# Two mixture-of-experts layers of sixteen experts: from computing every expert to computing sorted 128-slot blocks

## The reference, cut to what matters

```
router_logits = x @ gate_w.T                      # 16 experts
topk_w, topk_idx = top_k(softmax(router_logits), 4)
combine = one_hot(topk_idx) * topk_w / sum(topk_w)
shared = (silu(x @ sg.T) * (x @ su.T)) @ shared_down.T * sigmoid(x @ shared_gate_vec.T)   # inner width 704
for e in range(16):                               # inner width 176 each
    h = silu(x @ g[e].T) * (x @ u[e].T)
    acc += (h @ d[e].T) * combine[:, e]
x = x + 0.5 * (shared + acc)
```

## Time and profile before

| | |
|---|---|
| three runs | 1092.65, 1092.97 and 1095.82 us, median 1092.97 |
| span of the profiled execution | 1092.5 us; the page gives no other time of that execution |
| busy | PE 1010.5, DVE 800.6, ACT 384.8, POOL 465.1 us |
| DMA | 27.38 MB, mean 25 GB/s |
| mean granted TensorE clock | 0.987 |

### The profile page before, as it was taken

How to read it: one execution, slowest core, us unless ns; L and a number is a source line. 1 busy time by engine, 2 the same in 40 slices (tenths; PEclk the granted TensorE clock), 3 DMA queues, 4 the chain that set the end, 5 groups by cost and what they waited for, 6 DMA issues and landing times.

```text
span 1092.5 us, 18432 instructions
## 1 busy us (share of the span) xinstructions
PE 1010.5 (92%) x6692; PEld 584.0 (53%) x6692; DVE 800.6 (73%) x1429; ACT 384.8 (35%) x615; POOL 465.1 (43%) x373
## 2 busy tenths in 40 slices
PE   3989999899899899899799999999999999999997
PEld 1546555455555455555356555554455544555554
DVE  6887776967876967878977786466888778885444
ACT  1223223366423356422232332324432344322332
POOL 3646743466523456525466622231342313422222
PEclk8989999999999999999999999999999999999999
DMA  5212310000000000001233100000000000000000
GB/s 172 87 59 88 101 59 1 1 1 1 1 1 1 1 1 2 1 1 53 64 108 102 44 1 1 0 1 1 1 1 1 1 1 1 1 1 20 1 0 19
DMA packets 11814, 27.38 MB, mean 25 GB/s; under 512 B 1720, under 2 KB 4024, under 8 KB 11744
## 3 DMA queue, kind: packets, MB, share of 16 engines
q1 hardware_dynamic: 11744, 26.44, 8.1%
HBM read 25.38 MB, written 1.05 MB: 24 GB/s over the span
## 4 chain that ended last, share of the span: by engine, by line
PE 51%; DVE 28%; issue 10%; POOL 7%; ACT 3%; DMA 1%; SPq 0%; DVEq 0%; POOLq 0%; ACTq 0%
PE ps L719 28%; PE ps L748 12%; DVE hid L935 4%; POOL hlo L515 3%; DVE hid L937 3%; DVE hid L931 3%; PE ps L730 3%; PE ps L861 2%; POOL scr L554 2%; DVE scr L1119 1%; PE ps L795 1%; PE ps L760 1%; DVE combine L1041 1%; DVE scr L1112 1%; DVE picked L1024 1%
## 5 line engine op out<-in xcount | busy, mean ns | idle before, releaser
L515 POOL TENSOR_TENSOR hlo<-hid,hhi 128x512 f16<-128x512 f32 x208 | 252.2, 1212 | 566.5 <-ACT hhi L592 566.5
L719 PE MATMUL ps<-xhi,whi 128*128 128x512 f16 x832 | 319.7, 384 | 26.1 <-DVE hid L931 25.6
L719 PE MATMUL ps<-xhi,wlo 128*128 128x512 f16 x832 | 319.2, 384 | 0.0
L719 PE MATMUL ps<-xlo,whi 128*128 128x512 f16 x832 | 319.1, 384 | 0.0
L592 ACT ACTIVATE hhi<-hid 128x512 f16<-128x512 f32 x208 | 130.9, 629 | 464.9 <-DVE hid L937 464.7
L931 DVE SCALAR_TENSOR_TENSOR hid<-gtanh,ps 128x512 f32<-128x512 f32 x208 | 142.2, 684 | 174.1 <-ACT gtanh L585 159.6
L748 PE MATMUL ps<-whi,hhi 128*128 128x256 f16 (+1 forms) x832 | 227.7, 274 | 0.8 <-POOL hlo L515 0.8
L748 PE MATMUL ps<-whi,hlo 128*128 128x256 f16 (+1 forms) x832 | 227.3, 273 | 0.0
L748 PE MATMUL ps<-wlo,hhi 128*128 128x256 f16 (+1 forms) x832 | 227.1, 273 | 0.0
L935 DVE TENSOR_TENSOR hid<-hid,ps 128x512 f32<-128x512 f32 x208 | 143.0, 687 | 61.0 <-PE ps L730 56.1
L585 ACT ACTIVATE gtanh<-ps 128x512 f32<-128x512 f32 x208 | 123.3, 593 | 104.7 <-PE ps L719 104.4
(11 more groups left out here) (164 smaller groups left out, 927.4 us busy)
## 6 DMA issues: line engine op xcount, KB each, us to landing
stage<-w_in SPq DMA_DIRECT2D x58, 384.0 KB, 3.1
out<-x SPq DMA_DIRECT2D x2, 512.0 KB, 3.1
sel<-sel_in SPq DMA_DIRECT2D x1, 672.0 KB, 7.7
sel<-sel_in SPq DMA_DIRECT2D x2, 288.0 KB, 3.6
x<-x_in SPq DMA_DIRECT2D x4, 128.0 KB, 2.6
x<-x_in SPq DMA_DIRECT2D x1, 512.0 KB, 8.4
const<-const_in SPq DMA_DIRECT2D x1, 128.0 KB, 2.4
rw<-rw_in SPq DMA_DIRECT2D x1, 64.0 KB, 2.2
```

The source lines that it names most:

```text
L515: pool.tensor_tensor(hlo[:, k, :], hid[:, k % 2, :], hhi[:, k, :], ALU.subtract).then_inc(lo_done, 1)
L719: mm = pe.matmul(ps[:, bank, :], w[:, ds(off, P)], a[:, kc, t0:t0 + HN], start=(n == 0), stop=(n == 3 * KC - 1))
```

## The change

The sixteen experts of L0 are no longer computed for all tokens. For each half (512 tokens, 4 experts each, 2048 pairs) the kernel sorts pairs by expert into slots: an expert gets as many blocks of 128 slots as it needs, and 31 blocks always hold them (`NBLK`). The eight dense passes become twelve: "shared" passes of 6 chunks (the shared expert alone, dense as before but without the selection product), "routed" passes of 31 blocks, and four dense L1 passes of 24 chunks as before. Their order is shared(L0, half 0), routed(0), routed(1), shared(1); then, for the second L0, shared(0), routed(0), shared(1), routed(1); then the four L1 passes. They are called S0, R0, R1, S1, S2, R2, S3, R3 and F0 to F3 below.

On the way, in order: POOL and ACT split the normed rows (`xr`); DVE finds the four chosen experts (`route_pick`); PE counts with a triangle of ones the place of each pair within its expert (`rank`); DVE turns that into a slot number (`place`), into each block's expert (`block_experts`) and into each pair's weight (`slot_weights`); 16 indirect DMAs from POOL (4 experts x 4 tiles of 128 tokens, `send`) write the rows into `xs_dram`, which was blanked at the start; SP reads each block back with a transposing DMA, six ahead; PE reads the block's expert from memory into a register and computes gate and up with the block's slots as the stationary side; after the block's hidden values, two PE transposes, a copy on ACT and a difference on DVE (`turn`); six down products; a copy on ACT and a store to `ys_dram` by SP. At last 16 indirect DMAs from POOL (`gather`) fetch the four rows of each token back, and DVE adds them with their weights (`combine`).

```diff
+NBLK = HN * K0 // P + E0 - 1
+XRING, YRING, GRING = 6, 3, 4
-FFN_STAGES = (0, 2, 3, 5)
+PASSES = [(SH, 0, 0), (RT, 0, 0), (RT, 0, 1), (SH, 0, 1), (SH, 2, 0), (RT, 2, 0), (SH, 2, 1), (RT, 2, 1),
+          (F1, 3, 0), (F1, 3, 1), (F1, 5, 0), (F1, 5, 1)]
-GAPS = {PRE: 6}
+GAPS = {PRE: 3, 3: 5, 5: 4}
...
+        for n in range(4):
+            put(r, c + (2 + n) * step, "send", 4 * q + n)
...
+    def combine(q, r, c, step=1):
+        for n in range(4):
+            put(r, c + n * step, "gather", 4 * q + n)
+            put(r, c + (n + 1) * step, "combine", 4 * q + n, "A")
...
+    route0(2, 4, 0)
+    put(4, NSH - 1, "xs_first", 5)
+    c = combine(1, 4, 1)
...
+    for j in range(8):
+        put(7, 14 + 2 * j, "w1", j)
+    for j in range(8, WCH1):
+        put(8, (j - 8) // 2, "w1", j)
...
+                    pe.reg_load(at_expert[k], eoff[0:1, h, c:c + 1])
...
+                    pe.wait_ge(h_ready, u if c == 0 and PASSES[r - 1][0] != RT else u - 1)
+                    pe.wait_ge(xs_loaded[slot], 16 * xs_count(r, c))
...
+                    for kc in range(KC):
+                        for w, part in ((whi, 0), (whi, KC), (wlo, 0)):
+                            mm = pe.matmul(ps[:, m % 2, 0:2 * I0], xs_sb[:, slot, part + kc, :],
+                                           w[:, ds(offset[k] + (EXP0 + kc * 2 * I0), 2 * I0)],
+                                           start=(n == 0), stop=(n == 3 * KC - 1))
...
+                    for i in range(HT):
+                        pool.indirect_dma_start(out=xs_dram[h], out_offset=bass.IndirectOffsetOnAxis(
+                            ap=pos[:, h, j, i:i + 1], axis=0), in_=xr[:, i, :], in_offset=None,
+                            bounds_check=SLOT_ROWS - 1, oob_is_err=False).then_inc(sent[h], 16)
...
+                        if n:
+
+                            pool.wait_ge(combined, HT * (n - 1) + i + 1)
+                        pool.indirect_dma_start(out=back[:, i, :], out_offset=None, in_=ys_dram[h],
...
+                    for i in range(HT):
+                        dve.wait_ge(gathered[i], 16 * (n + 1))
+                        if j:
+                            dve.wait_ge(combined, HT * (n - 1) + i + 1)
+                        xb = x[:, HT * h + i, :]
+                        dve.scalar_tensor_tensor(out=xb, in0=back[:, i, :], scalar=wk[:, h, i, j:j + 1], in1=xb,
+                                                 op0=ALU.mult, op1=ALU.add).then_inc(combined, 1)
```

More of the change, by code:

```diff
@@ L466, in _, with load_block, chunk @@
-            sp_.wait_ge(x_added[1], added(ATTN_STAGE))
-            sp_.dma_start(heads, head_in).then_inc(heads_loaded, 16)
+            def load_block(r, b):
+                m, h = BLOCK[r] + b, PASSES[r][2]
+                k = b % XRING
+                sp_.dma_start_transpose(xs_sb[:, k, :, :], xs_dram[h][b * P:(b + 1) * P, :])\
+                    .then_inc(xs_loaded[k], 16)
+            def chunk(r, c, k, side):
+                side("A")
+                if PASSES[r][0] == RT and c + XRING < NBLK:
+                    sp_.wait_ge(gate_ready, UNIT[r] + c + 1)
+                    load_block(r, c + XRING)
@@ L468, in _ @@
+            run(None, chunk, piece, None, down)
             sp_.wait_ge(heads_loaded, 16)
@@ L594, in piece, with turn @@
-            def piece(name, n):
-                if name == "ln_hi":
+                if PASSES[r][0] == RT:
+                    return
+                act.wait_ge(h_ready, u + 1)
+                if not (isinstance(c, int) and u < 4):
+                    act.wait_ge(down_done, u - 3)
+                act.activation(hhi[:, k, :], hid[:, k % 2, :], ACT.Copy).then_inc(hi_done, 1)
+            def turn(r, c, k):
+                u, m = UNIT[r] + c, BLOCK[r] + c
+                act.wait_ge(turned, m + 1)
+                act.wait_ge(down_done, u - 3)
+                act.activation(hhi[0:IH, k, 0:2 * P], ps[0:IH, T_BANK, 0:2 * P], ACT.Copy)\
+                    .then_inc(hi_done, 1)
@@ L700, in _ @@
-            pe.wait_ge(act_consts, 1)
-            pe.wait_ge(pool_consts, 4)
-            def chunk(r, c, k, side):
-                t0 = HN * (r % 2)
-                if isinstance(c, int) and c == 0:
-                    pe.wait_ge(x_lo, ln_of(stage_of(r), r % 2))
-                if r in (0, 4):
-                    pe.wait_ge(w_split, c + ((WCH0 if r else 0) + 1))
-                first = isinstance(c, int) and BASE[r] + c == 0
-                for part, bank, free in ((0, G_BANK, act_done), (1, U_BANK, h_ready)):
+            pe.wait_ge(consts_loaded, 64)
@@ L712, in chunk @@
                     if not first:
[L714 removed]
+                        pe.wait_ge(free, u)
                     n = 0
@@ L731, in chunk, with turn @@
+                pe.matmul(ps[:, F_BANK, :], sel[:, ds(c * P, P)], cT[:, f % 2, :], start=True, stop=True)\
                     .then_inc(up_ready, 1)
-            def down(r, c, k):
+            def turn(r, c, k):
+                u, m = UNIT[r] + c, BLOCK[r] + c
+                pe.wait_ge(h_ready, u + 1)
+                pe.wait_ge(lo_done, u)
+                for j in range(2):
+                    mm = pe.transpose(ps[0:IH, T_BANK, P * j:P * j + P], hid[:, k % 2, IH * j:IH * (j + 1)], ident)
+                mm.then_inc(turned, 1)
@@ L893, in piece @@
                     mm.then_inc(outp_done, 1)
-            chunk.eng = pe
-            run(chunk, piece, down)
+            run(pe, chunk, piece, turn, down)
         @block.vector
```

837 lines of the change are left out of this document (592 added, 245 removed).

## The result

The changed kernel takes 1322.4 us (median of 4 runs, 1318.6 to 1326.0); the kernel before takes 1092.8 in the same runs. The ratio is 1.209, with a 95% interval of 1.205 to 1.212. The forecast was 1187, with a range of 1085 to 1300: the sign was right, the size was not. The profiled execution has a span of 1318.9 us.

A forecast was written before the change was run, and what follows sets the result against it. PE's stream was taken to bound the old kernel, POOL's issues and gather landings the new shared slots. S0 to R3 with gaps +46 and F0 +48 gave 1092.5 + 94 = 1186.5, forecast 1187 us, range 1085 to 1300.

The forecast's parts named there:

- a serial loop of POOL, landing and DVE in the gather slots: S2, S3: next chunk's DVE work waits for lo part, issues, landing and addition; 6.6 us plus 4g or 8g a slot.
- F0's gather slots: Four gather rounds in F0: those slots take 15.1 us instead of 4.1, within 150 us for F0, +48.
- g: POOL's time for issuing one send or gather, taken as 1.0 us, between 0.43 and 2.6.
- Issues cost POOL next to nothing: Rival: POOL hands an indirect DMA on at 0.1 us; 1107 with blocks at 2.25, 1085 at 1.82; chance 0.12 for faster.
- dear issues: Rival: DVE and POOL hold each other up when descriptors are written, g is 2, time 1299 us; chance 0.13.
- the transposing DMAs pace the blocks: Rival: each routed block waits for its transposing DMA; 1255 us at 3.1 us a block, 1330 at 4; chance 0.10.
- quiet blocks: Routed blocks without other work: 2.25 us each, from 1.82 us of PE plus one pause of 0.43; 31 make 70 us.
- six slots of 3.9 + 2 x 0.83 = 5.6 us: S1: each slot costed by PE, dense work plus two score units of 0.83; S1 45 us in all.
- my own rule: A slot lasts as long as its busiest engine, unless one must finish before another may start; then the chain counts.
- R3: 70 + 11 = 81: R3: 31 blocks at 2.25 us give 70, plus 11, so 81 us.
- 651 against 605: Passes S0 to R3 with gaps take 651 us, against 605 for L0 and attention before: +46.
- 88 us from the smaller dense work: Dense work falls from 461 to 373 us, so 88 us are won, against 182 lost elsewhere.

The follow-up runs named there:

- e1: Changed kernel with DVE's addition of each gather round placed behind the slot's own DVE work instead of ahead of it: 1273.3 us, ratio 1.164.
- e6: Changed kernel with R0's four send rounds meant to stand further apart; all engines' programs stayed the same, so a second measurement of it: 1306.2 us, ratio 1.194.
- e3: Changed kernel with the loads of the L1 weight pieces issued ahead instead of in the slot where ACT converts them: 1285.3 us, ratio 1.176.
- e2: Changed kernel with the score units of S1 placed in the order of the kernel before: 1292.4 us, ratio 1.183.
- e8: Changed kernel with old score order, early weight loads, additions later, half 1's gathers moved from S2 into S1, F0's gathers and weight pieces spread: 1163.1 us, ratio 1.064.
- e9: Changed kernel without sends and gathers (routed experts' part left out), with old score order and early L1 weight loads: 1075.8 us, ratio 0.984.
- e4: Changed kernel with filler products on PE where it waits (S1, S2, S3, starts of R0, R2, R3) to raise the granted clock: 1325.4 us, ratio 1.213.

## Why the prediction was wrong

**What held.** The sign, and the mechanism: a serial loop of POOL, landing and DVE in the gather slots (15.8 us against 14.6; S2, S3 and their ends 157 against 146; e1 showed each link), R1 108.3 against 108, F0's gather slots 14.9 against 15.1, the ends of the passes as waits of PE for xs_sb, and PE at 0.47 to 0.56 busy in S2, S3 and the first slots of F0. g was 1.28 and not 1.0: the term was mis-sized by a quarter. "Issues cost POOL next to nothing" is out by the rows of L701; "dear issues" by the same rows, and "the transposing DMAs pace the blocks" by blocks of 2.0 us. Two of the rivals' times came near to the result, 1330 (blocks of 4 us) and 1299 (dear issues), both for reasons that the rows exclude: luck.

Some of the good agreement is luck too. R0 is 84.5 us without its stall (e6) and R3 81.0 without its wait (e3), against 85 and 81. But the quiet blocks came at 2.03 us in the mean (blocks 20 to 30 of R0) where I had 2.25, 7 us less in a pass, so the work beside them took about 7 us more than my terms for it.

**S1, 41 us over.** The step that failed is "six slots of 3.9 + 2 x 0.83 = 5.6 us". It took a slot for its busiest engine, though my own rule was that the chain counts where an engine must finish before another may start. The order in the slot makes ACT, POOL and PE wait for each other once per slot; e2, by that order alone, took 35 us off S1 (30 off the whole) and left 28.0 us for its first five slots, just what the sum has for them. The other 5 lie in the last slot of S1 and the chain behind it: 27.3 us in e2, where my sum had 5.6 + 11.7 + 5 = 22.3.

**R3, 39 us over.** The step is "R3: 70 + 11 = 81". It had no term for the weight pieces that the change moves into R3: their load is issued in the slot in which it is needed. e3 gave back 37 (R3 itself fell from 119.6 to 81.0).

**F0, 19 over.** Ten of these come from the marks of my sum. Up to R3 its passes run from first product to first product, but the 605 us of before and the 102 of pass 4 are read between DVE's additions, and an addition comes 8.5 to 9.5 us after the first product of the next pass. The first products of the old passes 4 and 5, then that of F1 and the addition that ends F0:

```profile
608.48 0.38 PE L719 MATMUL ps<-xhi,whi 128*128 128x512 f16 x1
711.99 0.38 PE L719 MATMUL ps<-xhi,whi 128*128 128x512 f16 x1
```

```profile
938.38 0.38 PE L996 MATMUL ps<-xhi,whi 128*128 128x512 f16 x1
...
946.91 1.28 DVE L1271 SCALAR_TENSOR_TENSOR x<-ps,x 128x512 f32<-128x512 f32 x2
```

From its first product to its addition (720.5) the old pass 4 is 112 us and not 102; "651 against 605" should have been 651 against 595, and the same terms then give 1197. The other 9 are F0's own. Four slots took 14.8 to 15.2 as forecast, but the four behind them in which there are two weight pieces and no gathers took 5.3 to 6.2 and once 8.8, where I had at most 5.1. POOL's 1.15 + 2 x 1.64 and ACT's 4 x 0.84 + 0.60 + 0.63 are each over 4.1 already. One piece in a slot made it 4.8 (e8).

**R0, 15 over.** The stall, for which no row of before stood; 14 us from pass to pass (208.5 against 194.1). **S0 and the start, 16 over.** I let S0 start at 13 us, where the old pass 0 did; xlo, for which the first product waits, stands in DVE's queue behind a weight piece of 2.25 us and is done at 20.0. And S0's last slot and end took 24.5 us where the sum had 7.9 + 5: POOL is behind PE there. At 57.6, when PE's last gate products run, it still has two lo parts, four weight pieces and eight sends to do, up to 75.8. PE waits 18 us for xs_sb, and 22 to 23 at the other two ends.

**The gain that is left.** I had 88 us from the smaller dense work. e9 leaves 18 with all sends and gathers gone. The 88 compared slots with slots. From first product to first product, S0 to R3 take 543 us in e9, 52 less than the old passes 0 to 3; F0, which now holds weight pieces of L1, gives 21 of these back, and the later start 7. In e9 S0 with its end still takes 43 us, where six slots of 3.9 are 23: I read this as short passes that don't cover the routing, layernorms and weight pieces that the long ones did. I had part of these in the terms, on the losing side, and so the 182 lost and the 88 won can't be checked apart; their difference of 94 came out as 226 in the spans. The 31 blocks of a pass are the worst case that its shapes allow; how many of them held rows was not tried.

What stays open: why the unbroken row of issues goes with a stop of PE in some series of runs and not in others, and whether the chip decides it; and which share of the layernorm chains is POOL's and which DVE's.

## What to carry to other kernels

Before costing a slot by its busiest engine, write out who waits for whom inside it: the two largest errors here were visible in the order of the program's rows, without a single new price. When work is moved to a place where an engine is idle, look at what was queued behind it there; both moves of the gathers into or behind S1 cost more there than they saved in S2. And check that an edit changes the programs at all before a time is put down to it.

## What the hardware showed that I had not expected

A program identical on all engines ran in 1322.4 us in one series and in 1306.2 in another, both times within 0.8% over its four runs, and the traces show where: a stall of 16 us of PE beside a row of sixteen indirect DMA issues on POOL, and no packet of the instruction queues begins between 118 and 149 us (without the stall, two come near 136). All six kernels of one chip were without it, and on another chip breaking the row removed it in the one pair that can be compared. The granted clock was at 1.2 GHz for about a quarter of the span (its mean is 0.879, between the levels of 0.5 and 1) and cost nothing that e4 could find.
